# Moving the final waits for ten stores from SyncE's program to GpSimd's

## The chip, the cores and the metric

The kernel runs on one core of one Trainium2 chip. The metric is the device time of one execution in microseconds (us). Three runs of the kernel before took 986.73, 989.47 and 991.32 us; the median is 989.47 us.

## What is computed

The input `x` has 32 images of 384 channels of 64x64 fp32. It is normalized per group of 12 channels (32 groups to an image), each channel is shifted by the rounded offset of its position (48 positions, 8 channels each, offsets close to multiples of 16), blurred with a 3x3 Gaussian whose centre is the fraction of the offset, and added to `x`:

```
def _gn(v, G=32, eps=1e-5):
    g = v.reshape(B_, G, C_ // G, H_, W_)
    m = jnp.mean(g, axis=(2, 3, 4), keepdims=True)
    s = jnp.var(g, axis=(2, 3, 4), keepdims=True)
    return ((g - m) / jnp.sqrt(s + eps)).reshape(v.shape)

def _L0_conv_ref(inp, offset):
    off_round = jax.lax.stop_gradient(jnp.round(offset))
    out = _displace(inp, off_round.astype(jnp.int32))      # shift, zeros from outside
    frac = offset - off_round
    dx = field_x[None] + frac[:, None, None, 0]
    dy = field_y[None] + frac[:, None, None, 1]
    kern = jnp.exp(-(dx * dx + dy * dy) / (2.0 * SIGMA ** 2))
    kern = kern / jnp.sum(kern, axis=(1, 2), keepdims=True)
    ...                                                     # depthwise 3x3 convolution
x = x + _L0_conv_ref(_gn(x), L0_conv_offset)
```

## The kernel before

A tile is 128 rows of `x`, each a whole image plane of 4096 fp32: 16 images by the 8 channels of one position, 2 MB. There are 96 tiles (`ALL`): two chunks of 16 images by 48 positions. They pass through ten buffers, `tiles[:, n % 10, :]` (`SLOTS`), each with a semaphore for its load (`loaded`) and one for its store (`stored`). A semaphore of a buffer is at `landed(n)` when tile n's transfer is complete.

The engines run programs of their own, all inside one block. GpSimd issues every load (L184) and every store (L189) as an indirect DMA whose row numbers come from `row_of`. It issues ten loads, and then for each tile n waits until VectorE has finished it, issues its store, waits until the store of tile n-1 has landed, and loads tile n-1+10 into the buffer that came free (L195 to L202). From tile 87 on there is nothing left to load, and the last nine stores are issued with no wait for a store between them. ScalarE makes two passes over each tile for the sums of the statistics (L239, L243), TensorE adds them up over a group (L213), VectorE turns them into scale and shift, writes the normalized and shifted tile (L393), makes the two row taps (L409, L414) and the three column taps that add the result into the tile in place (L436, L434). The unit of the statistics is three tiles.

SyncE issues six small loads at the start (L171 to L176): the row numbers, the offsets in two layouts, the plan, the steps and the masks. After that it has only the ten waits at L178 and L179, one for each of the last ten stores (tiles 86 to 95, one for each buffer). Two semaphores share one instruction where they can.

When the programs have ended, the block ends (the profile gives this the line of `with ctx:`, L92): every engine has a DRAIN of its own, then reports by a semaphore, and the engines meet in a barrier (EVENT_SEMAPHORE). The same pair, DRAIN and EVENT_SEMAPHORE, stands at the start, in front of the block (L481). Nothing in the kernel's text places these instructions: an engine's DRAIN comes behind the last instruction of its program.

Of the kernel before, what the change touches and what calls it, by code (L numbers as in the profile page):

```python
# [29 lines left out]
ALL = CHUNKS * TILES  # L30
ALL_UNITS = CHUNKS * UNITS
SLOTS = 10
# [46 lines left out]
def norm_shift_blur(nc, x, offset, planned, steps, masks, rows, out):  # L79
# [12 lines left out]
    with ctx:  # L92
# [3 lines left out]
        def sem(name):  # L96
            return ctx.enter_context(nc.semaphore(name))
# [42 lines left out]
        stored = [sem(f"stored{s}") for s in range(SLOTS)]  # L140
# [24 lines left out]
        def landed(n):  # L165

            return (n // SLOTS + 1) * 16

        @block.sync
        def _(sp):  # L170
            sp.dma_start(row_of[:], rows).then_inc(rows_in, 16)  # L171
            sp.dma_start(offs[:], offset.unsqueeze(0).broadcast_to([128, NP, 2])).then_inc(tables_in, 16)
            sp.dma_start(plan_sb[:], planned).then_inc(tables_in, 16)
            sp.dma_start(offs_p[:], offset).then_inc(tables_in, 16)
            sp.dma_start(steps_sb[:], steps).then_inc(tables_in, 16)
            sp.dma_start(mask[:], masks).then_inc(masks_in, 16)  # L176

            for n in range(ALL - SLOTS, ALL):  # L178
                sp.wait_ge(stored[n % SLOTS], landed(n))  # L179

        @block.gpsimd
        def _(pool):
            def load(n):
                pool.indirect_dma_start(tiles[:, n % SLOTS, :], None, x_rows,  # L184
                                        bass.IndirectOffsetOnAxis(ap=row_of[:, n:n + 1], axis=0)
                                        ).then_inc(loaded[n % SLOTS], 16)

            def store(n):
                pool.indirect_dma_start(out_rows, bass.IndirectOffsetOnAxis(ap=row_of[:, n:n + 1], axis=0),  # L189
                                        tiles[:, n % SLOTS, :], None).then_inc(stored[n % SLOTS], 16)  # L190

            pool.wait_ge(rows_in, 16)
            for n in range(SLOTS):
                load(n)
            for n in range(ALL):  # L195

                pool.wait_ge(col_taps, 1 + (n + 1) * COL_TAPS)
                store(n)

                if n and n - 1 + SLOTS < ALL:  # L200
                    pool.wait_ge(stored[(n - 1) % SLOTS], landed(n - 1))
                    load(n - 1 + SLOTS)  # L202

        @block.tensor
        def _(pe):
# [280 lines left out]
```

## Time and profile before

| | |
|---|---|
| median of 3 runs | 989.47 us (986.73 to 991.32) |
| profiled execution | 984.86 us, of which its span 983.1 us |
| instructions in the span | 3636 |
| VectorE (DVE) busy | 871.3 us, 89% of the span |
| ScalarE (ACT) busy | 714.3 us, 73% |
| GpSimd (POOL) busy | 324.8 us, 33% |
| TensorE (PE) busy | 201.4 us, 20% |
| moved by DMA | 403.48 MB, 410 GB/s over the span |

The span is the time from the first to the last instruction of the profiled execution; the other 1.76 us of it lie around the span. Times in a trace are counted from the span's start. Engines are PE (TensorE), DVE (VectorE), ACT (ScalarE), POOL (GpSimd) and SP (SyncE). A name with a q behind it (POOLq, SPq) is the instruction sequencer of that engine: branches, semaphore instructions, DMA issues and DRAINs are there and are not counted as busy. L12 is line 12 of the kernel. An instruction that waits for a semaphore is shown from when the wait is over. `out<-tiles` means that `out` is written and `tiles` read.

### The profile page before, as it was taken

How to read it: one execution, taken by the hardware profiler on the slowest of the kernel's cores; microseconds unless marked ns; L12 is line 12 of the kernel's file. 1: busy time of each engine (PE TensorE's matmuls, PEld its weight loads, DVE VectorE, ACT ScalarE, POOL GpSimd, SP SyncE). 2: the span in 40 equal slices, each digit the busy share in tenths (PEclk: the TensorE clock that was granted, in tenths of full speed). 3: DMA queues.
4: the chain of work that ended last, by engine and by line, in shares of the span. 5: the costliest groups of instructions: out<-in, count | busy, mean ns of one | idle time of the engine just before them, and what ended most of it. 6: DMA issues, size and time to landing. Idle time of an engine off the chain costs nothing.

```text
span 983.1 us, 3636 instructions
## 1 busy us (share of the span) xinstructions
PE 201.4 (20%) x896; PEld 195.9 (20%) x896; DVE 871.3 (89%) x940; ACT 714.3 (73%) x412; POOL 324.8 (33%) x196
## 2 busy tenths in 40 slices
PE   0232222212122122122211221311212202222110
PEld 0221222212122122122211221311212202222110
DVE  4479899999999999999838949989999999979994
ACT  2998959777598777686777787686778777777800
POOL 3022342543323434223222317326141353223211
DMA  8999999999999999999999999999999999999966
GB/s 323 428 397 417 418 415 418 425 420 423 423 426 417 417 427 416 417 419 421 405 427 429 426 429 404 418 413 412 415 432 427 422 399 419 429 416 431 423 297 278
DMA packets 28233, 403.48 MB, mean 410 GB/s; under 512 B 3506, under 2 KB 3506, under 8 KB 3634
## 3 DMA queue, kind: packets, MB, share of 16 engines
q0 software_dynamic: 27648, 402.67, 98.2%
q1 hardware_dynamic: 562, 0.57, 0.2%
q8 instruction: 7, 0.11, 0.0%
q14 instruction: 16, 0.13, 0.0%
HBM read 201.90 MB, written 201.33 MB: 410 GB/s over the span
## 4 chain that ended last, share of the span: by engine, by line
DMA 54%; DVE 30%; issue 6%; POOL 5%; ACT 4%; PE 0%; POOLq 0%; ACTq 0%
DMA out<-tiles,row_of 48%; DVE tiles L434 10%; DMA tiles<-x,row_of 5%; DVE rowblur L409 5%; DVE tiles L436 5%; DVE rowblur L414 5%; POOL tiles L184 5%; ACT unread L239 3%; DVE normed L393 3%; ACT unread L243 1%; PE var_ps L213 0%; DMA row_of<-rows 0%; DVE scale L348 0%; DVE shift L351 0%; DVE apart L332 0%
## 5 line engine op out<-in xcount | busy, mean ns | idle before, releaser
L239 ACT ACTIVATE unread<-tiles 128x4096 uint8<-128x4096 f32 x94 | 339.9, 3616 | 165.2 <-DMA tiles<-x,row_of 164.7
L243 ACT ACTIVATE unread<-tiles,nmean_p 128x4096 uint8<-128x4096 f32 x94 | 348.7, 3709 | 3.0
L184 POOL DMA_INDIRECT tiles<-x,row_of x96 | 155.9, 1624 | 504.2 <-DMA out<-tiles,row_of 498.9
L434 DVE SCALAR_TENSOR_TENSOR tiles<-rowblur,ratio,tiles 128x272 f32<-128x272 f32 (+15 forms) x192 | 300.0, 1562 | 4.6
L213 PE MATMUL mean_ps<-nmean_p,mask 128*128 128x1 f32 x448 | 100.7, 353 | 567.3 <-ACT unread L239 537.2
L189 POOL DMA_INDIRECT out<-tiles,row_of x96 | 168.7, 1757 | 142.6 <-DVE tiles L434 119.7
L213 PEld LDWEIGHTS mean_ps<-nmean_p,mask 128*128 128x128 f32 x448 | 98.0, 330 | 570.0 <-ACT unread L239 539.8
L409 DVE SCALAR_TENSOR_TENSOR rowblur<-normed,ratio 128x272 f32<-128x272 f32 (+9 forms) x96 | 152.2, 1586 | 3.4
L436 DVE TENSOR_TENSOR tiles<-rowblur,tiles 128x272 f32<-128x272 f32 (+9 forms) x96 | 146.5, 1526 | 3.3
L414 DVE SCALAR_TENSOR_TENSOR rowblur<-normed,ratio,rowblur 128x240 f32<-128x240 f32 (+9 forms) x96 | 145.4, 1515 | 3.4
L213 PE MATMUL var_ps<-var_p,mask 128*128 128x1 f32 x448 | 100.7, 353 | 169.0 <-DVE var_p L338 169.0
L213 PEld LDWEIGHTS var_ps<-var_p,mask 128*128 128x128 f32 x448 | 98.0, 330 | 171.7 <-DVE var_p L338 171.7
L393 DVE TENSOR_SCALAR normed<-tiles,scale,shift 128x768 f32<-128x768 f32 (+6 forms) x96 | 87.3, 909 | 0.0
L251 ACT ACTIVATE std<-var_ps,eps 128x3 f32<-128x3 f32 x32 | 8.0, 252 | 50.8 <-PE var_ps L213 50.8
L329 DVE TENSOR_SCALAR nmean<-mean_ps 128x3 f32<-128x3 f32 x32 | 5.0, 155 | 37.2 <-PE mean_ps L213 37.2
L346 DVE RECIPROCAL rstd<-std 128x3 f32<-128x3 f32 x32 | 5.5, 171 | 27.1 <-ACT std L251 27.1
L312 DVE BATCH_NORM_STATS2 pieces<-tiles 128x6 f32<-128x512 f32 x16 | 9.7, 678 | 8.9 <-DMA tiles<-x,row_of 8.9
L239 ACT ACTIVATION_READ_ACCUMULATOR unread<-tiles 128x1 f32 x94 | 17.6, 187 | 0.0
L243 ACT ACTIVATION_READ_ACCUMULATOR unread<-tiles,nmean_p 128x1 f32 x94 | 17.5, 186 | 0.0
L390 DVE MEMSET normed<- 128x16 f32 (+3 forms) x96 | 8.5, 88 | 0.0
L338 DVE SCALAR_TENSOR_TENSOR var_p<-m_p,apart 128x3 f32<-128x3 f32 x32 | 5.2, 161 | 1.9 <-ACT unread L243 0.5
L351 DVE TENSOR_TENSOR shift<-scale,nmean 128x3 f32<-128x3 f32 x32 | 5.2, 164 | 1.1
(34 smaller groups left out, 25.9 us busy)
## 6 DMA issues: line engine op xcount, KB each, us to landing
tiles<-x,row_of POOLq DMA_INDIRECT x96, 14.9
out<-tiles,row_of POOLq DMA_INDIRECT x96, 17.6
mask<-masks SPq DMA_DIRECT2D x1, 448.0 KB, 3.2
row_of<-rows SPq DMA_DIRECT2D x1, 48.0 KB, 1.9
offs<-offset SPq DMA_DIRECT2D x1, 48.0 KB
plan_sb<-planned SPq DMA_DIRECT2D x1, 0.4 KB
offs_p<-offset SPq DMA_DIRECT2D x1, 0.4 KB
steps_sb<-steps SPq DMA_DIRECT2D x1, 12.0 KB
```

The costliest lines, as they stand in the source:

```text
L184: pool.indirect_dma_start(tiles[:, n % SLOTS, :], None, x_rows, bass.IndirectOffsetOnAxis(ap=row_of[:, n:n + 1], axis=0)).then_inc(loaded[ ...
L189: pool.indirect_dma_start(out_rows, bass.IndirectOffsetOnAxis(ap=row_of[:, n:n + 1], axis=0), tiles[:, n % SLOTS, :], None).then_inc(store ...
L213: last = nc.tensor.matmul(ps[:, k:k + 1], mask[:, PAIRS.index((j, k)), :], src[:, j:j + 1], start=(j == from_[0]), stop=(j == from_[-1]))
L239: nc.scalar.activation(unread[:], tiles[:, n % SLOTS, :], ACT.Identity, scale=-1.0 / HW, accum_out=nmean_p[:, i % 2, j:j + 1]).then_inc(nm ...
L243: nc.scalar.activation(unread[:], tiles[:, n % SLOTS, :], ACT.Square, bias=nmean_p[:, i % 2, j:j + 1], accum_out=m2_p[:, i % 2, j:j + 1]). ...
L312: nc.vector.bn_stats(pieces[:, e, :], tile[:, e, :]).then_inc(pieces_done, 1)
L390: nc.vector.memset(normed[:, 1 + ya:1 + yb, col:col + 1], 0.0).then_inc(edge_done, 1)
L393: nc.vector.tensor_scalar(normed[:, 1 + ya:1 + yb, 1 + xa:1 + xb], image[:, ya - oy:yb - oy, xa - ox:xb - ox], scale[:, i % 2, j:j + 1], s ...
L409: nc.vector.scalar_tensor_tensor(t[:, :, 1 + ea:1 + eb], g[:, :, 1 + ea + near:1 + eb + near], ratio[:, (near + 1) // 2, p, 0:1], g[:, :, ...
L414: nc.vector.scalar_tensor_tensor(t[:, :, 1 + fa:1 + fb], g[:, :, 1 + fa - near:1 + fb - near], ratio[:, (1 - near) // 2, p, 0:1], t[:, :, ...
L434: ins = nc.vector.scalar_tensor_tensor(y, t, ratio[:, (tap + 1) // 2, p, 1:2], y, ALU.mult, ALU.add)
L436: ins = nc.vector.tensor_tensor(y, t, y, ALU.add)
```

## The change

The ten waits move from the end of SyncE's program to the end of GpSimd's. After it, SyncE's program is its six loads, and GpSimd's last store is followed by the waits for stores 86 to 95. No transfer, no compute instruction and no other wait is changed.

```
--- before.py
+++ after.py
@@ -175,9 +175,6 @@
             sp.dma_start(steps_sb[:], steps).then_inc(tables_in, 16)
             sp.dma_start(mask[:], masks).then_inc(masks_in, 16)
 
-            for n in range(ALL - SLOTS, ALL):
-                sp.wait_ge(stored[n % SLOTS], landed(n))
-
         @block.gpsimd
         def _(pool):
             def load(n):
@@ -200,6 +197,9 @@
                 if n and n - 1 + SLOTS < ALL:
                     pool.wait_ge(stored[(n - 1) % SLOTS], landed(n - 1))
                     load(n - 1 + SLOTS)
+
+            for n in range(ALL - SLOTS, ALL):
+                pool.wait_ge(stored[n % SLOTS], landed(n))
 
         @block.tensor
         def _(pe):
```

## Rows read from the trace of the kernel before

**Rows 1.** The page: engines' busy time, DMA share and GB/s in 40 slices.

```profile
PE 201.4 (20%) x896; PEld 195.9 (20%) x896; DVE 871.3 (89%) x940; ACT 714.3 (73%) x412; POOL 324.8 (33%) x196
...
DMA  8999999999999999999999999999999999999966
GB/s 323 428 397 417 418 415 418 425 420 423 423 426 417 417 427 416 417 419 421 405 427 429 426 429 404 418 413 412 415 432 427 422 399 419 429 416 431 423 297 278
```

**Rows 2.** Waits of all engines: engine line waited for: us in total, times, longest.

```profile
POOL tiles L184 <- DMA out<-tiles,row_of: 498.9, 86, 9.4
...
POOL out L189 <- DVE tiles L434: 119.7, 21, 27.2
```

**Rows 3.** Chain that ended last, from 960 us: start, us, what.

```profile
962.34 1.05 DVE tiles L434
963.39 0.27 issue
963.65 1.28 POOL out L189
964.93 5.68 issue
970.61 1.18 POOLq L92
```

**Rows 4.** Instructions of L92, the block's end: duration ns min/median/max, start us.

```profile
L92 POOLq EVENT_SEMAPHORE  x2: 17/17/17, 982.9 to 982.9; - x2
L92 PEldq DRAIN  x1: 3130/3130/3130, 934.6 to 934.6; - x1
L92 ACTq DRAIN  x1: 274/274/274, 937.8 to 937.8; - x1
L92 POOLq DRAIN  x1: 12207/12207/12207, 970.6 to 970.6; - x1
L92 DVEq DRAIN  x1: 57/57/57, 972.4 to 972.4; - x1
L92 SPq COMPARE_BRANCH  x1: 33/33/33, 978.9 to 978.9; - x1
L92 SPq DRAIN  x1: 7/7/7, 979.0 to 979.0; - x1
...
L92 PEldq EVENT_SEMAPHORE  x1: 51/51/51, 983.0 to 983.0; - x1
```

**Rows 5.** Timeline from 934 us: start, us, engine, line, operation.

```profile
934.77 2.91 PE L213 MATMUL var_ps<-var_p,mask 128*128 128x1 f32 x13
937.78 0.26 ACT L251 ACTIVATE std<-var_ps,eps 128x3 f32<-128x3 f32 x1 [4.00 <-PE var_ps L213]
...
968.03 2.54 DVE L434 SCALAR_TENSOR_TENSOR tiles<-rowblur,ratio,tiles 128x960 f32<-128x960 f32 x2
970.85 0.95 POOL L189 DMA_INDIRECT out<-tiles,row_of  x1 [5.91 <-DVE tiles L434]
```

**Rows 6.** DMA issues from 965 us: median us from issue to landing at the end.

```profile
out<-tiles,row_of POOLq DMA_INDIRECT x1, 7.9
```

**Rows 7.** Instructions of L179, the ten waits on SyncE.

```profile
L179 SPq EVENT_SEMAPHORE  x5: 17/28/28, 950.5 to 978.8; - x5
```

**Rows 8.** SyncE's waits: engine line waited for: us in total, times, longest.

```profile
SPq L179 <- DMA out<-tiles,row_of: 975.3, 5, 947.2
```

**Rows 9.** Stretches: bounds, length, busy time of each engine, clock, DMA share, GB/s.

```profile
971.80:978.80 7.00, 0.00 (x0) 0.00 (x0) 0.00 (x0) 0.00 (x0) 0.00 (x0) 1.00 0.72 301
978.80:983.10 4.30, 0.00 (x0) 0.00 (x0) 0.00 (x0) 0.00 (x0) 0.00 (x0) 1.00 0.00 0
```

**Rows 10.** Instructions of L481, in front of the block.

```profile
L481 SPq DRAIN  x1: 7/7/7, 0.0 to 0.0; - x1
...
L481 POOLq DRAIN  x1: 188/188/188, 0.3 to 0.3; - x1
...
L481 POOL MEMSET const-uint8-127<- x1: 119/119/119, 0.3 to 0.3; 128x1 uint8 x1
```

**Rows 11.** Instructions that write `out`: duration ns, start; DMA from issue to landing.

```profile
L189 POOL DMA_INDIRECT out<-tiles,row_of x96: 950/1530/3861, 42.5 to 970.8; - x96
...
DMA to landing us min/median/max: 7.0/17.6/21.1
```

More of the change, by code:

```diff
@@ L176, in _ @@
             sp.dma_start(mask[:], masks).then_inc(masks_in, 16)
-            for n in range(ALL - SLOTS, ALL):
-                sp.wait_ge(stored[n % SLOTS], landed(n))
         @block.gpsimd
@@ L202, in _ @@
                     load(n - 1 + SLOTS)
+            for n in range(ALL - SLOTS, ALL):
+                pool.wait_ge(stored[n % SLOTS], landed(n))
         @block.tensor
```

## The prediction

> **What bounds the kernel now.** I read the page first. DVE is busy 89% of the span and the DMA engines nine tenths or more of nearly every slice, until the last two slices, where they are at six tenths [rows 1]. The waits say how these two share the middle: GpSimd waits 498.9 us, in 86 pieces, for a store to land before it can load into its buffer, and only 119.7 us for VectorE [rows 2]. So the middle goes at the pace of the transfers. The change touches no transfer and no instruction there, and I take the middle as given. What it touches comes after the last store, so the rest of the reading is the last 21 us.
>
> The chain of waits ends with VectorE's last column taps, the last store on GpSimd, and then a piece "POOLq L92", which is GpSimd's DRAIN at the block's end, not SyncE's waits [rows 3]. That is the first thing to see: the end isn't where the ten waits stand. The instructions of L92 give the order. GpSimd's DRAIN starts at 970.6 and takes 12.207 us, so it ends at 982.8; its two semaphore instructions stand at 982.9, those of the other engines at 983.0, and the last takes 0.051 us, which makes the span of 983.1 [rows 4]. SyncE passes its last wait at 978.8, branches at 978.9, and drains at 979.0 in 0.007 us [rows 4, 7]. It then stands ready for about 4 us, until GpSimd reports. The other three engines were ready earlier still, the last of them, VectorE, by 972.5 [rows 4].
>
> When was the last data down? The last store is issued at 970.85 and lands 7.9 us later, at 978.75 [rows 5, 6]; that agrees with SyncE's last wait. In the stretch from 978.8 to the end nothing moves and no engine is busy: DMA share 0.00, 0 GB/s, all busy times zero [rows 9]. Yet GpSimd's DRAIN is still running for 4.0 us of it. So the last 4 us of the kernel are a DRAIN with no visible object, and today it has run since 970.6, beside the last transfer.
>
> **The change, part by part.**
>
> Removed from SyncE: ten waits in five or six instructions of 0.017 to 0.028 us each [rows 7]. They took 975.3 us in all, of which 947.2 in one piece, but nobody was behind them except SyncE's own DRAIN and the barrier [rows 8]. SyncE will reach the barrier some microseconds after its sixth load instead of at 979.0. It wasn't last (979.0 against 982.8), so this is worth nothing.
>
> Added to GpSimd: the same waits, behind its last store. The first nine of these stores were issued before 965 us; the last to land is the last to be issued, at 978.75. Ten waits that have come true one by one cost GpSimd 5 or 6 x 0.03 = under 0.2 us, beside the last transfer, and one of 0.03 us on the path. No load or store is queued behind them. What is queued behind them is GpSimd's DRAIN, and for that one all engines wait at the barrier. This is the change's only real term: the DRAIN, which started at 970.6 while the last store was in flight, can now start only at 978.75 + 0.1 to 0.2 (SyncE's own steps from landing to the start of its DRAIN took 0.2) = 978.9.
>
> The price of the DRAIN from there isn't shown by the trace, since the one execution of it overlapped the transfer. Its bounds:
>
> - Below: GpSimd's other DRAIN, in front of the block, took 0.188 us, behind memsets of some 0.12 us and with no DMA issued before it [rows 10]. With that, GpSimd would be through at 979.1.
> - In the middle: 982.8 - 978.75 = 4.05 us, if all that the DRAIN does of its own begins when the last data is down.
> - Above: the whole 12.2 us, if the DRAIN's own work began with its record; or 11.0 us, if it began when the instruction ahead of it on GpSimd, the last store, had ended: 970.85 + 0.95 = 971.80 [rows 5], and 982.82 - 971.80 = 11.02.
>
> Which one? The DRAINs of the others show what a DRAIN does as to its own engine: TensorE's starts at 934.6, takes 3.13 us, and ends at 937.7, with the last matmul (934.77 + 2.91 = 937.68); ScalarE's takes 0.274 us around an activation of 0.26 us; VectorE's, with nothing in flight, 0.057 us [rows 4, 5]. They end 0.1 us or less behind their engine's last instruction. GpSimd's ended 11.0 us behind its last instruction and 4.05 us behind its last landing. A DRAIN that only waited for the engine would have ended at 971.9, one that only waited for the landings at 978.9. Neither fits, so there is work of its own in it, of at least 4.05 us. The simplest account of that is work that goes with the number of transfers GpSimd has issued in this kernel (192, against none at the first DRAIN), done entry after entry once the last store's instruction has ended, without regard to a landing that came 4 us before the end. I take 11.0 us, the row's time from the end of the instruction ahead. Spread over 192 entries it would be 0.057 us each.
>
> What the trace shows: a store's instruction is done in 0.95 to 3.9 us, and its data lands 7.0 to 21.1 us from issue [rows 11], so the record of the instruction isn't the transfer, and a semaphore is what tells of the landing. The Trainium skill (DMA: Bandwidth & Descriptors, section "Why a DMA increments its semaphore by 16 and not by 1") says that once the full 16 have arrived all the data has landed; a DRAIN that has to see transfers complete would then have nothing left to see behind these waits, and by that reading the kernel would end at 979.4. The 4.05 us behind the landing speak against it [rows 4, 6]. The Trainium skill (Perfetto Trace Analysis, section "Sequencer-only Instruction (DRAIN, etc)") says that such an instruction's record holds its execution and not its wait for a semaphore; by that the 12.2 us are execution, and all of them would come behind the waits, for an end at 991.4.
>
> The sum, in the profiled execution: last landing 978.75, start of the DRAIN 978.95, its end 978.95 + 11.02 = 989.97, barrier as now 983.05 - 982.82 = 0.25, so a span of 990.2 against 983.1: +7.1 us. With the 1.76 us around the span that execution would take 992.0 instead of 984.86. The runs shown are slower than the profiled one, with a median 4.6 us above it; the difference of 7.1 us is at the end and has nothing to do with what spreads them. So 989.5 + 7.1 = 996.6 us.
>
> **The rivals.**
>
> 1. The tail hangs on the landing (no change). The DRAIN's work of its own begins when the last transfer is down, and takes 4.05 us wherever the DRAIN is put. Then it ends at 978.95 + 4.05 = 983.0, the span is 983.2, and the median 989.6. For it: it needs no coincidence in the 4.05 us. Against it: the other engines' DRAINs end at once behind what they wait for.
> 2. A DRAIN that finds all complete is short (faster). If the 4.05 us are the coarse grain of its looking, or a handling that GpSimd's DRAIN only does for transfers that were in flight when it began, the waits would have let everything end before it. Then it costs about 0.2 us as at the start [rows 10], and ends at 979.15; the span is 979.4, 3.7 us less, and the median 985.8. The point from which this decides is a DRAIN of under 3.9 us from 978.95. For it: the short first DRAIN. Against it: that one had no transfer behind it at all, done or not.
> 3. The full record moves (slower by more): 12.2 us from 978.95 is 991.15, span 991.4, +8.3 us, median 997.8. It differs from my forecast by whether the DRAIN was already at work while the last store's descriptors were made (970.6 to 971.8).
>
> That the change doesn't do what it says would need a DRAIN that isn't behind the waits in GpSimd's program. SyncE's DRAIN stands behind its waits (979.0 against 978.8) [rows 4, 7], so I give it no chance of its own; its time would be that of rival 1.
>
> **How the numbers follow.** Forecast (DRAIN of about 11 us behind the waits) 0.50, the full record 0.08, tail on the landing 0.20, short DRAIN 0.22. The forecast and rival 3 lie at 996.6 to 997.8, and with the scatter of the runs (986.7 to 991.3 around 989.5, so some 2 us to either side of a median) 994.4 to 999.5. They hold 0.58; the range has to reach down over rival 1 (989.6, with scatter 987.5) to hold nearly 8 in 10, and a part of rival 2 (985.8 plus up to 2) is in it from 987.0. So 987.0 to 999.5. Beside it the likeliest case's own range is 994 to 999.5.
>
> Half a per cent, 4.95 us, is about what a measurement of this kernel can tell from no change. Slower by more than that: nearly all of 0.58, less the cases in which scatter takes the 7.1 us under 4.95, 0.51. Faster by more: rival 2 gives 3.7 us, under the bound, and passes it only by scatter, 0.08. Within: 0.41.
>
> **What would show each step.** In the profile of the changed kernel SyncE's DRAIN stands at a few microseconds from the start, and the last wait record on POOLq at the landing of the last store. GpSimd's DRAIN starts 0.1 to 0.3 us behind the landing. Its duration decides: 10 to 12.3 us is my forecast or rival 3, about 4 rival 1, under 1 rival 2. The transfers of the middle, the waits of [rows 2], and the 7 to 8 us of the last store should be as before; if the last store lands much later or earlier, that is scatter of the execution and not the change. I would be wrong if the DRAIN's time depends on what is still in flight, and wrong in size if it goes with the transfers outstanding and not with all issued, since the waits leave none outstanding.

## The result and the profile after

Over 22 runs of each kernel, taken in turn, the changed kernel took 989.32 us at the median (984.2 to 994.51) and the one before 985.53 (980.6 to 991.32). The ratio is 1.0035, with a 95% interval of 1.0018 to 1.0052: it is slower, by 3.4 us (1.8 to 5.1), half of what was forecast and less than half a per cent. The median of before is 4 us under that of the three runs shown ahead of the prediction, so only the ratio is used below.

The profiled execution of the changed kernel took 985.97 us with a span of 984.2. The spans of two single executions differ by other things than the change (its last store came 3.2 us earlier than in the trace of before), so what counts is the time from the last landing to the end. This is the block's end in the changed kernel: instructions of L92, with duration in ns and start in us.

```profile
L92 POOLq EVENT_SEMAPHORE  x2: 17/17/17, 984.0 to 984.1; - x2
L92 SPq DRAIN  x1: 122/122/122, 3.3 to 3.3; - x1
...
L92 DVEq DRAIN  x1: 57/57/57, 969.3 to 969.3; - x1
L92 POOLq COMPARE_BRANCH  x1: 33/33/33, 975.7 to 975.7; - x1
L92 POOLq DRAIN  x1: 8068/8068/8068, 975.9 to 975.9; - x1
```

Against [rows 4]: SyncE drains at 3.3 instead of 979.0, and GpSimd's DRAIN starts at 975.9 in place of 970.6 and takes 8.068 us in place of 12.207. These are the waits, which have moved to L202, and the last store with its time to landing:

```profile
L202 POOLq EVENT_SEMAPHORE  x5: 17/43/43, 967.4 to 975.6; - x5
```

```profile
967.68 0.95 POOL L186 DMA_INDIRECT out<-tiles,row_of  x1 [5.92 <-DVE tiles L434]
```

```profile
out<-tiles,row_of POOLq DMA_INDIRECT x1, 7.9
```

The store is issued at 967.68, lands 7.9 us later at 975.6, the last wait is over at 975.6 and the DRAIN starts 0.26 us behind the landing. That part of the path is as in [rows 5 to 7]. What stands behind the landing is the DRAIN alone. The stretches from the end of the last store's instruction to its landing, and from there to the end (bounds, length, busy time of the engines, clock, DMA share, GB/s):

```profile
968.60:975.60 7.00, 0.00 (x0) 0.00 (x0) 0.00 (x0) 0.00 (x0) 0.03 (x1) 1.00 0.72 301
975.60:984.20 8.60, 0.00 (x0) 0.00 (x0) 0.00 (x0) 0.00 (x0) 0.00 (x0) 1.00 0.00 0
```

The second is the stretch of [rows 9], with 8.60 us of nothing where there were 4.30. So the trace puts the change at +4.3 us, inside the interval of the runs.

8.07 us is none of the prices that the prediction had (0.2, 4.05, 11.0 and 12.2). It is nearly twice 4.05, and the experiments start from that.

### The profile page after: what moved, and what is told of

Same layout as the page of the kernel before. It is cut to its first block, busy times and chain, and to the rows that moved or that the text cites. A ratio compares the mean times of both kernels' runs of the same rounds, so it can differ in the third digit from the quotient of the medians.

```text
span 984.2 us, 3636 instructions
## 1 busy us (share of the span) xinstructions
PE 201.4 (20%) x896; PEld 195.9 (20%) x896; DVE 871.4 (89%) x940; ACT 714.4 (73%) x412; POOL 323.9 (33%) x196
## 4 chain that ended last, share of the span: by engine, by line
DMA 69%; DVE 15%; POOL 7%; issue 5%; ACT 3%; POOLq 0%; ACTq 0%; DVEq 0%
DMA out<-tiles,row_of 64%; POOL tiles L181 6%; DVE tiles L434 6%; DMA tiles<-x,row_of 5%; DVE rowblur L409 3%; DVE tiles L436 3%; DVE rowblur L414 3%; ACT unread L239 2%; DVE normed L393 1%; ACT unread L243 1%; POOL out L186 0%; DMA row_of<-rows 0%; DVE scale L348 0%; DVE shift L351 0%; DVE rstd L346 0%
## 5 line engine op out<-in xcount | busy, mean ns | idle before, releaser
L181 POOL DMA_INDIRECT tiles<-x,row_of x96 | 160.3, 1670 | 516.3 <-DMA out<-tiles,row_of 510.9
L186 POOL DMA_INDIRECT out<-tiles,row_of x96 | 163.4, 1702 | 128.2 <-DVE tiles L434 105.1
L332 DVE TENSOR_TENSOR apart<-nmean,nmean_p 128x3 f32<-128x3 f32 x32 | 5.3, 164 | 1.1
```

## Experiments

```diff
-    nc = bacc.Bacc("TRN2", target_bir_lowering=False, num_devices=1)
+    nc = bacc.Bacc("TRN2", target_bir_lowering=False, num_devices=1, dynamic_dma_scratch_size=4096)
```

```diff
-ALL = CHUNKS * TILES
-ALL_UNITS = CHUNKS * UNITS
+ALL = 48
+ALL_UNITS = ALL // UNIT
```

> The changed kernel with 48 of the 96 tiles left out (the second half of the images isn't computed), so 96 transfers are issued by GpSimd in place of 192. The DRAIN at the end, behind all landings: theory C (all transfers issued): 8.07 x 96 / 192 = 4.0 us. Theory F (fixed): 8.07 us. Theory R (entries still in the ring): between 4.0 and 8.07 us, by how many entries the ring holds; 8.07 if it holds 96 or fewer, 4.0 if it holds 192 or more.

The same with `ALL = 12`:

> The changed kernel with 84 of the 96 tiles left out, so 24 transfers are issued by GpSimd. The DRAIN at the end: theory C: 8.07 x 24 / 192 = 1.0 us. Theory F: 8.07 us. Theory R: 24 entries in the ring; with e2 it gives the time of an entry and with it how many the ring holds at the end of the full kernel (2.0 us here would say 96).

The DRAIN at the end of each, first with the quarter ring, then with 96 transfers, then with 24:

```profile
L92 POOLq DRAIN  x1: 2270/2270/2270, 976.9 to 976.9; - x1
```

```profile
L92 POOLq DRAIN  x1: 7905/7905/7905, 498.4 to 498.4; - x1
```

```profile
L92 POOLq DRAIN  x1: 2020/2020/2020, 157.1 to 157.1; - x1
```

A fixed price falls (2.02 us with 24 transfers, 2.27 with a small ring). All transfers issued in the program falls too: 96 give 7.905 us, nearly the 8.068 of 192. From 24 and 96, one transfer costs (7.905 - 2.020) / 72 = 0.0817 us and the rest is 0.06 us. By these, the full kernel's DRAIN has (8.068 - 0.06) / 0.0817 = 98 transfers in it, and that of the quarter ring (2.270 - 0.06) / 0.0817 = 27. So the DRAIN works through entries that are still in the ring, though every one of these transfers has landed; by this sum the ring of 16384 bytes held 98 of them at the end, and that of 4096 held 27.

The time of e1 was 1.0003 of before (0.9985 to 1.0021), where 2.5 us less than before was expected. One part of the miss is a subtraction: its DRAIN ends 2.53 us behind the landing (0.26 to its start, 2.27 of DRAIN), which is 1.5 us under the 4.05 of before and not 2.5. A ratio of 0.9985, which is what 1.5 us would make, is the lower end of the interval. Whether more than scatter is behind the rest isn't shown; the small rings below bear on it.

To see whether an entry costs by its bytes, each of the twelve stores of e3 was issued as two (the row table gets the numbers of half rows):

```diff
-                pool.indirect_dma_start(out_rows, bass.IndirectOffsetOnAxis(ap=row_of[:, n:n + 1], axis=0),
-                                        tiles[:, n % SLOTS, :], None).then_inc(stored[n % SLOTS], 16)
+                for h in range(2):
+                    m = (1 + h) * ALL + n
+                    pool.indirect_dma_start(out_halves, bass.IndirectOffsetOnAxis(ap=row_of[:, m:m + 1], axis=0),
+                                            tiles[:, n % SLOTS, h * HW // 2:(h + 1) * HW // 2], None
+                                            ).then_inc(stored[n % SLOTS], 16)
```

> The kernel of e3 (84 of 96 tiles left out, waits on GpSimd) with each of its 12 stores issued as two, of half the bytes each: 12 loads and 24 stores, 36 transfers in place of 24, the same bytes. If the DRAIN goes by transfers: 36 x 0.082 + 0.06 = 3.0 us behind the waits. If it goes by bytes: 2.02 us as in e3.

```profile
L92 POOLq DRAIN  x1: 3000/3000/3000, 157.6 to 157.6; - x1
```

3.000 us, as 36 transfers give it: the same bytes in more transfers cost more, so the price isn't one of bytes. Each transfer, whole or half, still has 128 rows and 144 packets (3456 packets on GpSimd's queue in e3, 5184 here), so these runs don't tell a price of a transfer from a price of its rows; 0.0817 us holds for a transfer of 128 rows.

### Why 4.05 us when the DRAIN starts early

First, which of the ten waits costs. Only the last store's wait goes back to SyncE:

```diff
             sp.dma_start(mask[:], masks).then_inc(masks_in, 16)
 
+            sp.wait_ge(stored[(ALL - 1) % SLOTS], landed(ALL - 1))
+
...
-            for n in range(ALL - SLOTS, ALL):
+            for n in range(ALL - SLOTS, ALL - 1):
                 pool.wait_ge(stored[n % SLOTS], landed(n))
```

> The changed kernel with one wait of the ten, that for the last store, put back at the end of SyncE's program; the other nine stay on GpSimd. Theory P (what the change costs is that the DRAIN can't start before the last store has landed, the other nine waits come true before GpSimd is through with the last store's instruction): the DRAIN starts as in the kernel before, ends 4.0 to 4.1 us behind the last landing, and the time is that of the kernel before (ratio 0.998 to 1.002). Rival Q (waits on GpSimd as such make its DRAIN later or longer): the DRAIN ends about 8.3 us behind the last landing and the time is that of the changed kernel (ratio 1.0035).

```profile
L92 POOLq DRAIN  x1: 11342/11342/11342, 968.4 to 968.4; - x1
L92 SPq COMPARE_BRANCH  x1: 33/33/33, 975.7 to 975.7; - x1
```

The DRAIN starts at 968.4 and ends at 979.7, 4.05 us behind the landing at 975.65: the end of before is back, with nine waits still on GpSimd. The ratio to before is 1.0018 (0.9995 to 1.0040), which overlaps the expected range (0.998 to 1.002) but also holds the changed kernel's 1.0035, so the times decide nothing here; the trace does.

Then the two halves. A memset behind GpSimd's last store puts the DRAIN's own work off while nothing else changes. Short and long, in the kernel before, each run once for its trace:

```diff
                     load(n - 1 + SLOTS)
 
+            nc.gpsimd.memset(normed[:, 0:30, :], 0.0)
```

> The kernel before, with one GpSimd memset of 128x1980 fp32 behind the last store, so that the DRAIN's own work begins some 2 us later. Theory H: the first pass (4.0 us from the memset's end) is still over before the last landing, and the DRAIN ends 4.0 to 4.1 us behind the landing as without the memset. Rival M: its end moves by the memset's length, or by that less one pass of 3.7 us. Rival W (8.07 us of work in one piece, of which what is left at the landing follows it, and the 4.05 us were a chance of when it began): the end moves by the memset's length.

```diff
+            nc.gpsimd.memset(normed[:], 0.0)
```

> As e7 with a memset of 128x4356 fp32, so that it ends some 4 to 9 us behind the last store's instruction. Theory H: the DRAIN ends at the later of the memset's end + 4.03 us and the last landing, plus 4.05 us; if the memset ends more than 3 us behind the last store's instruction, the end is 8.07 us behind the memset's end. Rival M: a whole number of passes of 3.7 us behind the memset's end.

The memset of the first, its DRAIN, and SyncE's branch behind the landing:

```profile
970.67 1.77 POOL L204 MEMSET normed<- 128x1980 f32 x1
```

```profile
L92 POOLq DRAIN  x1: 12212/12212/12212, 969.5 to 969.5; - x1
L92 SPq COMPARE_BRANCH  x1: 33/33/33, 977.7 to 977.7; - x1
```

and of the second:

```profile
969.67 3.74 POOL L204 MEMSET normed<- 128x4356 f32 x1
```

```profile
L92 POOLq DRAIN  x1: 13002/13002/13002, 968.5 to 968.5; - x1
L92 SPq COMPARE_BRANCH  x1: 33/33/33, 976.7 to 976.7; - x1
```

With the short one the landing is at 977.67 and the DRAIN ends at 981.72, 4.05 us behind it: a delay of 1.8 us has cost nothing. With the long one the memset ends at 973.41, 3.74 us behind the store's instruction (a little less than the 4 us aimed at, and over the 3 us from which it should count), the landing is at 976.66, and the DRAIN ends at 981.49, 8.08 us behind the memset and 4.83 behind the landing. Two halves, as expected, give 973.41 + 4.03 = 977.44 for the end of the first, which is later than the landing, and with 4.05 for the second the measured 981.49. One piece of work that moves with its start, and looks of a fixed grain (rival M), both miss the first of these runs, and M the second too (8.08 is no whole number of 3.7).

So the DRAIN's end is the later of (start of its own work + half) and the last landing, plus the other half, where a half is 0.041 us times the entries in the ring, plus about 0.04 us. What the two halves are inside GpSimd, no run here shows; that the first can run while a transfer is in flight and the second can't is what the traces of before, e4 and the two memsets share.

### What follows: empty the ring, or keep it small

If the second half is what before pays, a smaller ring shortens it. Here with the waits on SyncE, as before, at a quarter and at an eighth (`dynamic_dma_scratch_size=2048`) of the ring:

> The kernel before (waits on SyncE), with the descriptor ring of GpSimd's DMAs at 4096 bytes of a partition in place of 16384. Theory H (the DRAIN is two passes over the entries in the ring, of equal length; the first can run beside a transfer in flight, the second begins at the last landing): its end lies half of e1's 2.27 us, 1.1 to 1.2 us, behind the last landing, against 4.05 us with the full ring, so the kernel is 2.9 us shorter than before (ratio 0.997). Rival M (the DRAIN looks at what is in flight in passes of a fixed length near 3.7 us, three of which end where it ended): 0 to 3.7 us behind the landing, by chance.

> As e5 with a ring of 2048 bytes of a partition. Theory H: half of 1.1 us, 0.5 to 0.7 us behind the last landing, 3.4 us shorter than before (ratio 0.9965), if so small a ring holds up no transfer; if it does, GpSimd's issue instructions in the middle take longer than the 1.5 us of median they took, or come later, and the time is longer than that of e5.

GpSimd's DRAIN and SyncE's branch behind its last wait, first of the quarter and then of the eighth:

```profile
L92 POOLq DRAIN  x1: 9307/9307/9307, 976.9 to 976.9; - x1
L92 SPq COMPARE_BRANCH  x1: 33/33/33, 985.1 to 985.1; - x1
```

```profile
L92 POOLq DRAIN  x1: 8709/8709/8709, 975.3 to 975.3; - x1
L92 SPq COMPARE_BRANCH  x1: 33/33/33, 983.6 to 983.6; - x1
```

The DRAIN ends 1.15 us and 0.58 us behind the landing, as expected of half the work of 27 entries (2.27 / 2) and of half as many. That also rules out a last stretch of a fixed length. The quarter ring's ratio to before is 0.9966 (0.9942 to 0.9990), 3.3 us less, where 2.9 was expected. The eighth's is 1.0009 (0.9986 to 1.0032): its end is the shortest and its time is not. The traces show one thing in the middle that goes with it. From the landing of the store that a load waits for (or the end of GpSimd's instruction ahead, where that is later) to the start of the load, the median of the 86 loads is 0.26 us in before and 0.50 us in the eighth ring; with the quarter ring it is 0.26 with single ones of 0.61, a mean of 0.30. That is 86 x 0.24 = 21 us of later loads in the one and 86 x 0.04 = 3 us in the other, part of which the other buffers can hide. It fits that a full ring is cleared at issue in place of at the end, but no run isolates it, so the 4 us that the eighth ring gave back (3.4 us less than before were expected, 0.9 us more were measured) are argued and not shown. In e1, with its quarter ring, the mean is 0.30 us too; but the quarter ring with the waits on SyncE has the same late loads and still gained what was expected of it, so the rest of e1's miss stays open.

The other way is to empty the ring where GpSimd has nothing to do. It waits 13.1 us for VectorE between the stores of tiles 91 and 92. The edit, once in the kernel before and once in the changed one:

```diff
                 store(n)
+                if n == ALL - 5:
+                    pool.drain()
```

> The kernel before (waits on SyncE, full ring) with one more DRAIN in GpSimd's program, behind the store of tile 91, where GpSimd waits 13.1 us for VectorE in the trace of before. Theory H (a DRAIN takes the entries of completed transfers out of the ring for good): the added one ends 4.05 us behind the landing of store 91, about 1 us after store 92 could go, which the transfers ahead of the last store absorb; the last one finds 4 entries, 4 x 0.082 = 0.3 us in all, and ends 0.1 to 0.3 us behind the last landing in place of 4.05. The kernel is 3.7 to 3.9 us shorter than before (ratio 0.996). Rival (each DRAIN pays for all transfers issued so far, or for the whole ring): the last one takes as long as before and the time is that of before or more.

> As e10 with the ten waits on GpSimd, as in the changed kernel. Theory H: the DRAIN at the end stands behind the last landing with 4 entries and takes 0.3 to 0.4 us, so the place of the waits costs 0.3 to 0.5 us against e10 in place of 4.3, and the kernel is 3.3 to 3.5 us shorter than before (ratio 0.9965). Rival: 8 us, ratio 1.0035.

With the waits on SyncE, the added DRAIN, GpSimd's stores around it, and the block's end:

```profile
L200 POOLq DRAIN  x1: 16572/16572/16572, 939.5 to 939.5; - x1
```

```profile
939.71 1.95 POOL L189 DMA_INDIRECT out<-tiles,row_of  x1 [9.32 <-DVE tiles L436]
956.79 1.33 POOL L189 DMA_INDIRECT out<-tiles,row_of  x1 [15.13 <-issue]
959.14 1.15 POOL L189 DMA_INDIRECT out<-tiles,row_of  x1 [1.03 <-DVE tiles L436]
```

```profile
L92 POOLq DRAIN  x1: 8546/8546/8546, 971.9 to 971.9; - x1
L92 SPq COMPARE_BRANCH  x1: 33/33/33, 980.3 to 980.3; - x1
L92 SPq DRAIN  x1: 7/7/7, 980.5 to 980.5; - x1
```

The added DRAIN ends at 956.05, 3.88 us behind the landing of store 91 at 952.16, where 4.05 was expected; the full ring less the four stores not yet issued is 94 entries, and half of their work is 94 x 0.041 + 0.04 = 3.9 us. The store of tile 92 goes at 956.79 after an idle time of 15.13 us; in before it was 13.12. This one store is 2 us late, where about 1 was expected. The one of tile 93 comes 1.03 us behind it, and from there VectorE sets the pace again: the last store is issued 32.4 us behind that of tile 91 in both traces. At the end GpSimd's DRAIN is over at 980.47, 0.21 us behind the landing at 980.26, and before SyncE's at 980.5: now SyncE is the last. For four entries the rule gives 4 x 0.041 + 0.04 = 0.20. The ratio to before is 0.9966 (0.9949 to 0.9983), 3.3 us less.

With the waits on GpSimd:

```profile
L92 POOLq COMPARE_BRANCH  x1: 38/38/38, 976.1 to 976.1; - x1
L92 POOLq DRAIN  x1: 381/381/381, 976.3 to 976.3; - x1
```

Four entries at 0.0817 and 0.06 us make 0.387; the row has 0.381. The end is 0.65 us behind the landing, and the ratio to before 0.9954 (0.9936 to 0.9971). The intervals of the two overlap for the most part, so the place of the ten waits no longer makes a difference that these runs can see: with four entries left, the change is worth 0.65 - 0.21 = 0.4 us by the traces. Both are faster than the kernel before by a third to half of a per cent, and so faster than the changed one too.

## Why the prediction was right and wrong

- **Where the end is.** Right. The ten waits were not the end; GpSimd's DRAIN was, and the rest of the kernel is unchanged by the edit [rows 3, 4].
- **What the removed waits are worth.** Right: nothing. SyncE drains at 3.3 us and nobody notices.
- **What the added waits do.** Right in mechanism: of the ten one counts, that of the last store (e4), and it puts the DRAIN's start behind the last landing. Start expected 0.2 us behind it, measured 0.26.
- **The price of the DRAIN.** This is the step that failed, the term of the DRAIN and the overlap in it. I took the 11.02 us from the end of the last store's instruction as one piece of work, and so the whole of it as moved. But the record holds a wait in its middle: 4.0 us of work beside the transfer, then about 3 us until the landing, then 4.05 us of work. Without the wait it is 8.07 us. The term of the sum was 11.0 us and measured 8.07; the forecast difference was +7.1 us and the trace's is +4.3, the runs' +3.4 (1.8 to 5.1).
- **The argument for one piece.** I argued that the DRAIN, ending neither with the store's instruction nor at the landing, had work of its own that ran without regard to the landing. Right that it had work of its own; the second part didn't follow. Rival 1 had the second half of the truth: 4.05 us do hang on the landing. It lacked the first half, which an early start hides and a late one doesn't. The truth lay between it and the forecast, and the prediction had no case there, though both were built from the same row. Its own sign, "I would be wrong if the DRAIN's time depends on what is still in flight", came true: half of the work doesn't begin before the landing.
- **A row misread.** I wrote that the other engines' DRAINs end 0.1 us or less behind their engine's last instruction. That holds for TensorE and ScalarE. VectorE's last taps end at 970.57 and its DRAIN at 972.49 [rows 4, 5], 1.9 us behind, so the row gave less ground for holding it against rival 1 than I took from it. (The barrier is 983.05 - 982.82 = 0.23 us, not 0.25; nothing changes by it.)
- **By what it goes.** I spread 11 us over the 192 transfers issued, 0.057 us each. It is 98 entries still in the ring at 0.082, by the sum from e2 and e3. The clause "wrong in size if it goes with the transfers outstanding" named the wrong thing: none was outstanding, and 98 entries of landed ones were.
- **The rules drawn on.** The Trainium skill (DMA: Bandwidth & Descriptors, "Why a DMA increments its semaphore by 16 and not by 1") holds as far as it goes: nothing moved any more behind the full semaphore (0 GB/s from 975.6 us on). The reading that a DRAIN then has nothing left was mine, and the 8.07 us refute it. The Trainium skill (Perfetto Trace Analysis, "Sequencer-only Instruction (DRAIN, etc)") gave the time of rival 3. The trace agrees that a wait for a semaphore is outside the record: the changed kernel's DRAIN starts 0.26 us behind the landing. But the record of 12.207 us held 4.1 us that weren't the DRAIN's own work, the store's instruction ahead and the wait for the landing, and they didn't move with it.
- **Chances.** Slower by over half a per cent had 0.51; 0.35% is within. The median of 989.32 us lies in the range of 987.0 to 999.5, but this is no merit of the sum, which gave 996.6. The range had been stretched down over rival 1 (989.6), whose mechanism isn't what happened either, and the nearness to that number is luck: over all its 22 runs the kernel before has a median 3.9 us under the 989.47 that the sum started from, which hides the 3.4 us that the change cost. From 989.47 it would have been 992.9, inside the range as well.

## What to carry to other kernels

The last instruction of GpSimd's program isn't the end of its work. When it has issued DMAs, its DRAIN at the block's end goes through every entry still in its ring, 0.082 us each for the indirect DMAs of 128 rows here, 8 us for 98, and half of that comes behind the last landing even when it starts early. Leave the waits for the last stores to an engine that has nothing to do, so that the first half runs beside the last transfer; and if the end matters, give GpSimd a DRAIN in an idle stretch shortly before it (3.3 us of 981 here, measured in this one kernel). When a record spans both a known event and work of unknown extent, price it as work before the event, wait, and work after, and keep a case for each split.

## What the runs showed of the hardware that I had not expected

- GpSimd's DRAIN costs by completed transfers: 2.020 us for 24, 3.000 for 36, 7.905 for 96, 0.381 for 4, and 8.068 after 192, which is the price of 98.
- Half of this (4.05 us of 8.07, 1.15 of 2.27, 0.21 of 0.38) stands behind the last landing however early the DRAIN begins, and the other half can run beside a transfer.
- A DRAIN takes the entries out for good: after one at 939.5 us, the next ended 0.21 us behind the last landing in place of 4.05, the price of the 4 transfers issued since.
- A ring of 2048 bytes in place of 16384 moved the loads from 0.26 to 0.50 us behind the landing that they wait for, and the kernel's time was that of before (1.0009), though its DRAIN ended 3.5 us closer to the last landing. That the late loads cost it this gain is not shown.
